# Small fills between GpSimd's scatters, and one deviation moved into its own tile, in a routed expert kernel

## What is computed

```python
def attn(x):                      # s: a complex decay per scale, summed along the sequence, then gated
    for i in range(2):
        b = (x @ W_re + b_re + 1j * (x @ W_im + b_im)) * (1.0 - r)
        _, h = jax.lax.associative_scan(_scan_op, (a, b), axis=1)
        h_scales.append(h.real)
    h = jnp.concatenate(h_scales, axis=-1)
    return jax.nn.sigmoid(h @ W_gate + b_gate) * h

def ffn(X):                       # f: the 2 best of 8 experts for each token
    topv, topi = jax.lax.top_k(X @ Wg + bg, 2)
    xs = X[:, :, None, :] * softmax(topv)[..., None]
    out = X
    for e in range(8):
        h = silu(xs @ W1[e]) * (xs @ W3[e])
        y = h @ W2[e]
        out = out + jnp.where((topi == e)[..., None], y, 0.0).sum(axis=2)
    return out
```

## Time and profile before

| | |
|---|---|
| runs | 316.03 us median of 3 (315.44 to 316.64) |
| the profiled execution | 315.75 us, of it 314.0 us span |
| TensorE busy | 289.3 us (92%) |
| VectorE, ScalarE busy | 230.4 us, 171.0 us |
| GpSimd busy | 149.1 us (47%), of it 69.5 us for 71 result scatters and 68.4 us for 64 row scatters |

### The profile page before, as it was taken

The page is one execution under the profiler, slowest core; times in us unless marked ns, Lnnn a source line. Parts: engine busy times, 40 slices in busy tenths (PEclk is TensorE's granted clock), DMA queues, the critical chain, the costliest instruction groups (busy, mean ns, idle before and its releaser), DMA issues.

```text
span 314.0 us, 6542 instructions
## 1 busy us (share of the span) xinstructions
PE 289.3 (92%) x1973; PEld 255.7 (81%) x1973; DVE 230.4 (73%) x614; ACT 171.0 (54%) x361; POOL 149.1 (47%) x172
## 2 busy tenths in 40 slices
PE   8885795999999999999999998999999999997983
PEld 8774754899987989889998888999999999786331
DVE  3898887998598795768776785786776777574086
ACT  2889557576255975466646654455455554442031
POOL 2448878677114666376656742234344343334010
PEclk9955599999999999999999999999999999999998
DMA  6959714036210151112419649759786834940696
GB/s 188 348 174 324 224 49 145 29 90 181 70 33 20 42 153 51 36 43 69 109 52 154 181 126 352 247 194 319 263 287 243 312 99 151 335 133 13 226 382 195
DMA packets 42797, 52.17 MB, mean 166 GB/s; under 512 B 5622, under 2 KB 33530, under 8 KB 40844
## 3 DMA queue, kind: packets, MB, share of 16 engines
q1 hardware_dynamic: 36428, 40.57, 41.8%
q0 software_dynamic: 4320, 8.43, 8.1%
q10 hardware_dynamic: 2016, 2.76, 2.5%
HBM read 22.20 MB, written 14.26 MB: 116 GB/s over the span
## 4 chain that ended last, share of the span: by engine, by line
PE 65%; DVE 13%; issue 6%; ACT 6%; DMA 4%; POOL 2%; SPq 1%; POOLq 0%; DVEq 0%
PE bank L1485 12%; PE bank L1429 5%; PE bank L1438 5%; PE bank L1431 5%; PE bank L1430 5%; PE bank L1469 4%; PE bank L1440 4%; PE bank L1439 4%; PE bank L1486 4%; PE bank L1220 3%; PE bank L1221 3%; PE bank L1222 3%; PE bank L1531 3%; DMA early<-in_L_attn_x 3%; PE bank L1405 2%
## 5 line engine op out<-in xcount | busy, mean ns | idle before, releaser
L551 POOL DMA_INDIRECT y_dram<-stage,row x71 | 69.5, 978 | 104.4 <-DVE stage L1153 89.9
L542 POOL DMA_INDIRECT rows_dram<-rows,slot_row x64 | 68.4, 1068 | 25.3 <-issue 15.0
L735 ACT ACTIVATE stage<-bank 128x512 f32<-128x512 f32 x71 | 42.4, 598 | 69.4 <-PE bank L1431 40.2
L1485 PE MATMUL bank<-ew,hid_t 128*128 x284 | 73.0, 340 | 1.3 <-DVE stage L1153 0.7
L1485 PEld LDWEIGHTS bank<-ew,hid_t 128*128 128x128 f32 x284 | 53.4, 188 | 1.7 <-issue 1.6
L748 ACT ACTIVATE hid_t<-bank 128x512 fp32r<-128x512 f32 x71 | 40.8, 598 | 10.6 <-PE bank L1469 7.9
L1137 DVE TENSOR_TENSOR stage<-bank,stage 128x512 f32<-128x512 f32 x41 | 28.1, 686 | 17.5 <-PE bank L1431 17.0
L1429 PE MATMUL bank<-ew,row_t_hi 128*128 x82 | 34.6, 422 | 4.7 <-DVE row_t_lo L1131 4.5
L1486 PE MATMUL bank<-ew,hid_t 128*128 x164 | 36.4, 222 | 0.0
L1137 DVE TENSOR_TENSOR bank<-bank,stage 128x512 f32<-128x512 f32 x30 | 21.0, 699 | 17.8 <-PE bank L1440 17.7
L1431 PE MATMUL bank<-ew,row_t_hi 128*128 x82 | 32.3, 394 | 0.0
(11 more groups left out here) (178 smaller groups left out, 703.4 us busy)
## 6 DMA issues: line engine op xcount, KB each, us to landing
u<-ew SPq DMA_DIRECT2D x10, 1024.0 KB, 5.0
mix<-ew SPq DMA_DIRECT2D x5, 1024.0 KB, 5.5
stage<-in_L_ffn_W SPq DMA_DIRECT2D x15, 256.0 KB, 4.9
early<-in_L_attn_x SPq DMA_DIRECT2D x7, 512.0 KB, 4.8
row<-rows_dram SPq DMA_DIRECT2D x41, 64.5 KB, 2.0
xn_dram<-early SPq DMA_DIRECT2D x4, 512.0 KB, 4.0
u<-xn_dram SPq DMA_DIRECT2D x4, 512.0 KB
ew<-y_dram SPq DMA_DIRECT2D x8, 256.0 KB, 6.9
```

The lines of the kernel that those rows point to most:

```text
L542: pool.indirect_dma_start(out=rows_dram[:, :], out_offset=bass.IndirectOffsetOnAxis(ap=slot_row[:, q % 2, at:at + 1], axis=0), in_=rows[:, ...
L551: pool.indirect_dma_start(out=y_dram[:, :], out_offset=bass.IndirectOffsetOnAxis(ap=row[:, k, D:ROW].bitcast(U32), axis=0), in_=y[:, t % Y ...
L735: act.activation(silu[:, t % 2], bank[:], ACT.Silu).then_inc(silu_done, 1)
L1485: pe.matmul(to, hi[:, at:at + P], w[c], start=(c == 0), stop=False, skip_group_check=True)
```

## The change

`pause()` fills three cells of a tile `unread` that nothing reads. Each cell is one number in each of the 128 partitions. It is called ahead of every second scatter, row scatters and result scatters counted together, in the loop over the tiles as long as `j` is below `FIRST_PAIR` (34). That makes 36 pauses for 72 scatters. Each pause but the first waits for a semaphore that the pause before it has raised. Besides, `inverse_deviation(2)` moves from ahead of the loop into tile 2.

```diff
-EACH = 2
+EACH, TOGETHER = 2, 2
...
+            def pause():
+
+                if pauses[0]:
+                    pool.wait_ge(paused, pauses[0])
+                for n in range(3):
+                    ins = pool.memset(unread[:, n:n + 1], 0.0)
+                ins.then_inc(paused, 1)
+                pauses[0] += 1
...
-            inverse_deviation(2)
+            went = [0]
+
+            def paced():
+
+                if went[0] % TOGETHER == 0:
+                    pause()
+                went[0] += 1
+
             for j in range(J + 1):
                 for t in range(TILE[j], TILE[j] + UNITS[j]) if j < J else ():
+                    for q, at in STATS_AT.items():
+                        if t == at + 2:
+                            inverse_deviation(q)
                     for q in ROWS_SENT:
                         for n in share(ROWS_SENT, q, t):
                             if n % HALF == 0:
                                 row_ids(q, n // HALF)
+                            paced()
                             scatter_row(q, n)
-                    for q, at in STATS_AT.items():
-                        if t == at + 2 and q > 2:
-                            inverse_deviation(q)
                 for d in sent_down(j) if j < J else (J - 2, J - 1):
+                    if j < FIRST_PAIR:
+                        paced()
                     scatter_result(d)
```

More of the change, by code:

```diff
@@ L193, in build @@
         keep_sum = sb("keep_sum", [P, E, GT + 1], F32)
-        half_power = sb("half_power", [P, GT], F32)
+        half_power, unread = sb("half_power", [P, GT], F32), sb("unread", [P, 3], F32)
         pad_row = sb("pad_row", [P, ROW], F32)
@@ L288, in build @@
         carry_done, count_ready, count_seen = sem("carry_done"), sem("count_ready"), sem("count_seen")
-        ids_done, row_done = sem("ids_done"), sem("row_done")
+        ids_done, row_done, paused = sem("ids_done"), sem("row_done"), sem("paused")
         sent = [[sem(f"sent{q}_{half}") for half in range(2)] for q in range(NG)]
@@ L555, in scatter_result @@
                         bounds_check=DUMP - 1, oob_is_err=False).then_inc(y_out[k], 16)
+            pauses = [0]
+            def pause():
[5 more added lines that the diff above has]
+                pauses[0] += 1
             inverse_deviation(0)
@@ L582, in _ @@
             inverse_deviation(1)
[L583 to L587, removed]
-            inverse_deviation(2)
+            for n in range(ROWS):
+                scatter_row(0, n)
+            row_ids(1, 0)
+            for n in range(HALF):
+                scatter_row(1, n)
+            went = [0]
[3 more added lines that the diff above has]
+                went[0] += 1
             for j in range(J + 1):
                 for t in range(TILE[j], TILE[j] + UNITS[j]) if j < J else ():
+                    for q, at in STATS_AT.items():
+                        if t == at + 2:
+                            inverse_deviation(q)
                     for q in ROWS_SENT:
```

## The result

The changed kernel takes 317.34 us in the median of 21 runs (316.54 to 321.58), against 316.03 us for 21 runs of the kernel before on the same chip: a ratio of 1.0044 (95% interval 1.0031 to 1.0058), so 1.4 us more (1.0 to 1.8). A few runs of most kernels here, the one before too, take 1.5 us or more above their median; the longest, 321.58 us, ran at the lowest granted clock (0.945) and isn't in the ratio. The page of the profiled execution begins with

The account below looks back on a forecast made before the run. TensorE, 92% busy, was taken to bound the kernel, with GpSimd's last scatter r15 setting tile 34 and the end. Two pauses of 0.17 us add 0.34 us, the deviation nothing: 316.03 + 0.34 = 316.4 us, range 314.9 to 318.6.

Parts of the forecast that it names:

- The sum: Whole kernel: r15, tile 34 and the end 0.34 us late, so the median 316.03 becomes 316.4 us.
- rival A: GpSimd's scatters: one behind a fill starts late, c = 0.64 us, backlog exceeds 4.7 us room; 322.2 us, chance 0.18.
- the port rule: VectorE, 85 to 105 us: GpSimd fills could block its small instructions through shared ports, 317.1 us; left out of the sum.
- a cause that none of these rows shows: Lone tiles: sign of a wrong forecast if their stretch shortens by more than TensorE's idle time; alternatively shorter products.
- Part 1, the pauses: GpSimd: 15 pauses fit the 4.7 us room before y27; two between y27 and r15 delay the end 0.34 us.
- c: GpSimd's added time per pause between scatters: taken as 0.17 us, bounds 0 and 0.30 us.
- The nearest row: GpSimd's writing of row numbers between scatters, model for a pause: 0.18 us, making the gap 0.45 instead of 0.30.
- rival C: GpSimd: fills vanish in the 0.30 us scatter gaps, c = 0, 316.0 us; chance 0.2, counted within the forecast's 0.75.
- Part 2, the deviation: Third group's deviation on GpSimd runs 62.19 to 63.86 us, 1.7 us before VectorE reads it; costs nothing.
- Rival B: Scatters and tile 34's load: spacing lets them land sooner, at most 1.7 us gained, 314.3 us; chance 0.07.

Follow-up runs that it names:

- experiment 2: The kernel before with an unused `unread` where the change has it, no pauses, deviation unmoved: 317.19 us, ratio 1.0033.
- Experiment 6: The kernel before with only `inverse_deviation(2)` moved into tile 2, no pauses, no `unread`: 316.11 us against 316.11, ratio 1.0002.
- experiment 7: The changed kernel with `unread` behind all other tiles and 16 fills a pause instead of 3: 320.37 us against 316.11 for the kernel before, 1.0134.
- experiment 1: The changed kernel with `unread` allocated behind all other tiles, pauses and moved deviation kept: 316.34 us against 315.91 for the kernel before, 1.0012.
- Experiment 5: The kernel before with 32 unused bytes directly ahead of `row_t_hi`, so `mix` stays: 316.84 us against 316.11, ratio 1.0030.
- experiment 3: The kernel before with an unused `unread` of 64 bytes instead of 12: 317.0 us against 315.91, ratio 1.0030.
- 11: The kernel before with `keep_sum` behind `h_bias`, plus pauses, moved deviation and `unread` behind all tiles; another chip: 340.23 us against 342.57, 0.9955.
- 12: The kernel before with `keep_sum` allocated behind `h_bias`, run again on another chip: 341.15 us against 342.57, ratio 0.9973.
- experiment 10: The kernel before with `keep_sum` (288 bytes) allocated behind `h_bias`, so `mix` moves down and `row_t_hi` stays: 315.46 us against 316.52, 0.9957.

## Why the prediction was right, and where not

**The result** lies in the range and on the side that had the most chance (within 0.5%, though the interval reaches to 0.58%), and the time is 0.9 us above the forecast. The sum had +0.34 us, and +1.4 us (1.0 to 1.8) came. **That it held is luck**: the range reached up to 318.6 us for rival A and the port rule, neither of which came, and a cost that the prediction did not have fell into it.

**The step that failed** stands in the change part by part. It priced the instructions that the change adds and moves, and had no term for the tile that it allocates: not one sentence asks what `unread` moves. The tile alone costs 317.19 - 315.91 = 1.3 us by the medians, or 1.0 us by its ratio (experiment 2), and 1.01 us of the loss stands in the pairs, which the prediction left aside since nothing of GpSimd changes there. It named "a cause that none of these rows shows" for the lone tiles only. Line L1438 lay in reach: in the trace of before, the products with `mix` already ran at 119.0 ns and those with `u` at 114.3, equal work at two speeds, and nothing asked why.

**Part 1, the pauses.** Bounds of c of 0 and 0.30 us held, the value taken did not: 0.02 to 0.03 us in front of a row scatter, not 0.17. The nearest row, numbers between scatters, was the wrong model: a fill runs in the 0.30 us between scatters, of which 0.16 us remain behind it. The numbers' instruction ended 0.28 us ahead of the scatter that waits for it. The prediction had named this as the lower bound, and rival C. Ahead of result scatters it is the same 0.33 us where nothing else holds them, as at 106.90 us. r15 is late by 0.16 us: 0.05 by the pauses, 0.11 since y27 is. Its landing was 0.31 us shorter and tile 34's load 0.38 us longer, and tile 34 starts 0.23 us late. TensorE's wait grew by 0.09 us.

**Part 2, the deviation,** went as written:

```profile
60.84 0.96 POOL L542 DMA_INDIRECT rows_dram<-rows,slot_row  x1 [0.16 <-issue]
61.83 1.68 POOL L525 TENSOR_TENSOR rstd<-var_eps,half_power 128x8 f32<-128x8 f32 x1
63.69 1.03 POOL L542 DMA_INDIRECT rows_dram<-rows,slot_row  x1 [0.19 <-issue]
```

It ran from 61.83 to 63.51 us (predicted 62.19 to 63.86), since the pauses are cheaper. VectorE read it at 65.52, as before, and nobody waited. Experiment 6 has it alone: no change.

**The port rule.** VectorE is busy 18.10 us in 85 to 105 us in both traces, with 13 GpSimd instructions there instead of 7. L1009, which was L988, takes 352 ns once and 159 ns in the median, as in the earlier trace rows. The Trainium skill's rule ("SBUF — State Buffer", section "Who interferes with whom") lets a GpSimd instruction hold up one of VectorE's in a two-port mode. The trace shows no cost of it here, where two pauses fall into the stretch, and leaving it out of the sum was right.

**Rival A** did not happen, since no scatter behind a fill starts over. Its arithmetic held when c was made large: experiment 7. **Rival B** didn't happen; landing was quicker once and the load slower, which is one execution's chance as far as these runs tell. **Rival C** describes GpSimd best: experiment 1, 1.0012 (0.9997 to 1.0028).

**Open.** Of the 1.29 us of the profiled span, 1.01 are in the pairs, 0.23 stand at tile 34 (0.09 of them its longer wait) and 0.05 come behind the pairs. The lone tiles' products are slower too: from L1429 to L1430 the mean is 230.0 ns before and 233.3 after, from L1430 to L1431 230.1 and 232.4, steps with a wait left out. There `row_t_hi` and `row_t_lo` are the weights, and the expert's weights in `ew` are streamed past them. Experiments 2 and 5, with `row_t_hi` 32 bytes up, have this slow-down as well, and experiment 3, 64 bytes up, has not (230.2 and 230.2). That it costs time isn't shown: from tile 9 to tile 34 it is 100.9 us before, 101.2 after and 100.9 in experiment 2. Tile 34 starts at 186.80 to 187.34 us in all executions but those of experiments 7, 11 and 12. Experiment 6, with all tiles in the places of before, has 186.80 where before had 187.11, so 0.3 us there say nothing. The physical reason of the pattern is open.

## What to carry to other kernels

Price a new tile as you price an instruction: look up where the tiles behind it stand before and after, even if the tile is 12 bytes and nobody reads it. An unused tile of the same size in the old kernel, and the new code with its tile behind all others, part the two causes in two runs. And if equal products of one line run at two speeds in the trace of before, find out why first: here it led, by one moved line of allocation, to a kernel 0.2 to 0.4% faster than the one before (experiment 10, on one chip; on another the interval includes no difference).

## What the runs showed of the hardware

The pace of TensorE's products at the full clock depends on the places of its two operands in a partition: 113.3 to 114.3 ns from start to start of 128x256 products where `row_t_hi` less the weights is 192 modulo 256 bytes, 118.4 ns at 224, 119.7 and 119.8 at 0, 117.8 at 64, 117.2 to 119.0 at 160. Experiment 5 shows it best, since `mix` doesn't move and its products gain 5.7 ns by 32 bytes elsewhere; its one pair at 118 ns shows that the distance isn't all. The tile of 12 bytes takes 32 bytes of each partition in the built program.

The Trainium skill ("TensorE: Matmul & The Clock Gate", section "Step-by-step: what each phase is for") says that the streamed operand and the weight load have read ports of their own, so that loading the next weights takes nothing from the running product. No trace here shows the two reads apart. Each product has a weight load of its own (1973 of each on the page), and its pace changes by up to 5% when either operand is moved against the other. If the two reads collide, which is the nearest reading but was not shown, the sentence doesn't hold in full; the measured paces decide, whatever the reason.

Three fills in 0.17 us between two of GpSimd's scatters cost 0.02 to 0.03 us: they run inside the 0.30 us that lie between scatters in any case, and 0.16 us remain behind the last of them.
